# GAT and mixture-of-experts kernel, edge loop: order of weighing, adding, softmax and rescaling

## What is computed

```python
h   = einsum('nf,hfo->nho', layernorm(x), W)
e_s, e_d = einsum('nho,ho->nh', h, a_src), einsum('nho,ho->nh', h, a_dst)
scores = leaky_relu(e_s[src] + e_d[dst], 0.2)
m   = segment_max(scores, dst)                      # per node and head
ex  = exp(scores - m[dst])
agg = segment_sum(ex / segment_sum(ex)[dst] * h[src], dst)
x1  = x + relu(agg)
out = x1 + experts(layernorm(x1))                   # top 2 of 8, gelu between two layers
```

## Time and profile before

| | |
|---|---|
| median of 3 runs | 1369.36 us (1367.18 to 1370.95) |
| the profiled execution, own time | 1363.46 us |
| its span, first to last instruction | 1361.6 us |
| mean granted clock of TensorE | 0.745 |
| busy over the span: PE, DVE, POOL, ACT | 54%, 55%, 55%, 32% |
| instructions | 11490 |

### The profile page before, as it was taken

The page is one execution under the profiler, slowest core; times in us unless marked ns, Lnnn a source line. Parts: engine busy times, 40 slices in busy tenths (PEclk is TensorE's granted clock), DMA queues, the critical chain, the costliest instruction groups (busy, mean ns, idle before and its releaser), DMA issues.

```text
span 1361.6 us, 11490 instructions
## 1 busy us (share of the span) xinstructions
PE 730.0 (54%) x2620; PEld 543.7 (40%) x2620; DVE 744.5 (55%) x1862; ACT 429.8 (32%) x1157; POOL 751.7 (55%) x801
## 2 busy tenths in 40 slices
PE   7800324434445445443454455444446658999990
PEld 5600213323333333333343343333334555767770
DVE  7502334566556645666566456646667785444445
ACT  5331021432243314332432243224333263222220
POOL 2577746666666666666666666667650003444430
PEclk9855657777776776667766766777778758999995
DMA  6343423333333333333333333333328221111217
GB/s 195 84 115 105 109 66 97 97 99 97 98 99 93 92 97 95 95 97 101 98 90 97 95 94 96 96 97 101 94 79 288 68 78 51 67 63 66 64 46 238
DMA packets 77549, 136.04 MB, mean 100 GB/s; under 512 B 21953, under 2 KB 50081, under 8 KB 77355
## 3 DMA queue, kind: packets, MB, share of 16 engines
q0 software_dynamic: 37344, 101.67, 27.4%
q1 hardware_dynamic: 37401, 30.76, 7.4%
q10 hardware_dynamic: 2738, 2.88, 0.7%
HBM read 119.41 MB, written 16.48 MB: 100 GB/s over the span
## 4 chain that ended last, share of the span: by engine, by line
issue 35%; PE 18%; PEld 15%; DVE 15%; PEldq 11%; another core or an unknown queue 2%; DMA 1%; SPq 1%; DVEq 0%; ACT 0%; POOL 0%; POOLq 0%; ACTq 0%
PEld psum L673 15%; PEldq L675 11%; PE psum L763 6%; PE psum L785 6%; DVE acc L1183 2%; PE psum L622 2%; PE psum L775 2%; PE psum L715 1%; PE psum L752 1%; DVE links L1213 1%; DVE C L1223 1%; PE psum L706 1%; DVE acc L1530 1%; DVE acc L1531 1%
## 5 line engine op out<-in xcount | busy, mean ns | idle before, releaser
L546 POOL DMA_INDIRECT ring<-h_tab,srcP x664 | 631.3, 951 | 312.1 <-issue 191.4
L673 PE MATMUL psum<-ring,shared 128*128 128x260 f32 x1328 | 437.5, 497 | 492.9 <-issue 444.1
L673 PEld LDWEIGHTS psum<-ring,shared 128*128 128x128 f32 x1328 | 327.2, 254 | 593.2 <-issue 470.4
L1183 DVE TENSOR_TENSOR acc<-acc,psum 128x260 f32 x332 | 140.4, 423 | 297.8 <-PEq L675 238.3
L881 ACT ACTIVATE shared<-iota_f,Dcol 128x128 f32<-128x128 f32 x664 | 202.2, 386 | 159.8 <-PEq L675 143.6
L1270 DVE TENSOR_TENSOR ring<-ring,psum 128x2048 f32<-128x2048 f32 x83 | 189.8, 2287 | 34.1 <-remote 21.6
L899 ACT ACTIVATE Ex<-Z 128x128 f32<-128x128 f32 x21 | 6.5, 309 | 459.6 <-DVE Z L1237 251.7
L556 POOL DMA_INDIRECT ring<-z_tab,ring x47 | 45.1, 959 | 132.6 <-DVE ring L1473 118.6
L886 ACT ACTIVATE shared<-shared,ones 128x1024 f32<-128x1024 f32 x83 | 95.3, 1148 | 42.5 <-remote 32.1
L983 ACT ACTIVATE RS_all<-psum,tail_consts 128x128 f32<-128x128 f32 x188 | 53.7, 368 | 144.8 <-PE psum L775 144.8
L562 POOL DMA_INDIRECT ys_tab<-shared,ring x47 | 46.1, 980 | 94.7 <-DVE shared L1501 94.7
(11 more groups left out here) (296 smaller groups left out, 701.6 us busy)
## 6 DMA issues: line engine op xcount, KB each, us to landing
ring<-h_tab,srcP POOLq DMA_INDIRECT x664
ring<-in_L_ffn_W SPq DMA_DIRECT2D x16, 512.0 KB, 9.9
h_tab<-ring SPq DMA_DIRECT2D x10, 260.0 KB
ring<-in_x SPq DMA_DIRECT2D x1, 2432.0 KB
z_tab<-ring SPq DMA_DIRECT2D x2, 1024.0 KB, 4.4
ring<-ys_tab SPq DMA_DIRECT2D x4, 512.0 KB, 9.2
ring<-ys_tab ACTq DMA_DIRECT2D x4, 512.0 KB, 9.8
out<-acc SPq DMA_DIRECT2D x4, 512.0 KB
```

The source lines that it names most:

```text
L546: pool.indirect_dma_start(out=ring[:, t % RING, :], out_offset=None, in_=h_tab, in_offset=bass.IndirectOffsetOnAxis(ap=srcP[:, t:t + 1], a ...
L673: pe.matmul(sums[G_at % NSUM][:, 0:MW], dst_oh[:, n % OHB, 2 * g + r, :], ring[:, t % RING, :], start=(r == 0), stop=(r == 1))
L1183: v.tensor_tensor(a, a, sums[(n * GB + g) % NSUM][:, 0:MW], ALU.add).then_inc(flushed, 1)
```

## The change

In DVE's program all four batches of a phase are weighed, and three of them added, before the softmax product of the next phase begins. The flush of the last batch goes behind the first weigh of the next phase. `rescale` goes behind the third weigh, with a wait of its own for the phase's first batch. `gates` has one flush and the rescaling less ahead of it. PE's factor product goes behind the fourth batch, and ACT makes one more batch of one-hots ahead of the exponents. No instruction of arithmetic is added or removed.

```diff
 (PE)
                 batch(n + 2)
+                batch(n + 3)
                 if f < NPH - 2:
                     factor(f + 1)
-                batch(n + 3)
 (ACT)
                 lay_seeds(f + 2)
+                one_hots(n + 4)
                 exponents(f + 1)
-                one_hots(n + 4)
                 one_hots(n + 5)
 (DVE)
                 weigh(n)
                 if f:
-                    flush(n - 2)
+                    flush(n - 1)
                 weigh(n + 1)
-                if f:
-                    flush(n - 1)
-                    rescale(f)
                 gates(f + 1)
                 weigh(n + 2)
+                if f:
+                    v.wait_ge(batch_done, n + 1)
+                    rescale(f)
                 flush(n)
+                weigh(n + 3)
+                flush(n + 1)
+                flush(n + 2)
                 if f < NPH - 2:
                     weights(f + 1)
-                weigh(n + 3)
-                if f < NPH - 2:
                     factor(f + 1)
-                flush(n + 1)
-                if f < NPH - 2:
                     turn(f + 1)
             last = (NPH - 1) * PB
-            flush(last - 2)
-            flush(last - 1)
             weights(NPH - 1)
             factor(NPH - 1)
             turn(NPH - 1)
             weigh(last)
+            flush(last - 1)
             v.wait_ge(fac_in, 1)
             rescale(NPH - 1)
```

## The result

The changed kernel takes **1373.04 us** (median of 14 runs, 1367.97 to 1376.78), the kernel before on the same chip **1369.45 us** (14 runs): ratio **1.002, 95% interval 1.0011 to 1.003**. A second comparison, at a later time, gave 1367.49 against 1362.73 us, 1.0024 (1.0006 to 1.0041). The change costs about 0.2%; the forecast was 0.3% the other way. It lies in the forecast's range, within what I called no change, but the term that made the forecast a gain (the start, -10) came to nothing, and the other two came out otherwise too.

A forecast was written before the change was run, and what follows sets the result against it. The edge loop was taken as paced by waits: PE's marks held while POOL's gathers run. +4 - 10 + 1.5 = -4.5 us gave 1359.0, plus 5.9 to the median, 1364.9 us; range 1332 to 1400.

The forecast's parts named there:

- the start, -10: Start of the edge loop: second batch's mark comes at 186.3 instead of 196.3, 3 us after POOL's last gather; -10 us.
- the hold: Edge loop: while gathers run, a second PE batch's mark is not released until POOL stands still; mechanism unknown.
- Rival (c): Start of the loop: its loss only moves with phase 1's softmax to the new place; 1374.9 or 1370.9 us, chance 0.11.
- Loop, +4 us: Softmax moved behind the third batch's flush: mean cost 0.2 us in 20 phases, +4 us, ends 0 and +44.
- T + 20.3 to 25.0: Next phase's first batch done 20.3 to 25.0 us after T, when a phase's third batch is done; cover until 22.8.
- rival (a): Edge loop: the serial softmax chain becomes the bound, +22 to +44 us, giving 1383 to 1405 us; chance 0.34.
- the pairs of 22.8 us: Edge loop's usual cycle: two batches in 20 us of gathers plus about 2.8 us of POOL standstill.
- Rival (b): Edge loop: late first batch isn't held, POOL stands 1 us instead of 3; -40 us, about 1325; chance 0.19.
- Removed stall: PE's mid-batch stop for sum banks, flush behind softmax, eight times (34.5 us): removal worth 0 inside the loop.
- Tail, +1.5 us: After the last gathers: third batch ends earlier, but the last softmax starts at 1050.4 instead of 1048.86; +1.5 us.
- Gates, rescale's new wait, factor, SP: 0: Edge loop: earlier gates, rescale's added wait, PE's later factor product and SP's earlier-released loads each cost 0.
- the 60 us of the Trainium skill's rule: PE idle gaps halve the clock: by the rule alone 3 us a phase, 60 us more; left out of the sum.

The follow-up runs named there:

- experiment 7: The changed kernel once more, unaltered, measured beside the kernel before at a later time: 1367.49 against 1362.73 us, ratio 1.0024.

## Why the prediction was wrong

**Start, -10 us: the step that failed.** I wrote that the hold would end "3 us after POOL's last gather (183.3)". The cover that I named, DVE's crawl, was taken away as predicted: DVE had nothing beside the second batch from 165.6 us on and the softmax of phase 1 took 8.8 us. The mark came at 195.9 all the same, and POOL's wait is 12.33 instead of 13.12. The 3 us were no constant but the backlog of 16 gathers; 88 gathers make 12 to 13 us. Both numbers were in front of me: 2.8 / 16 = 0.18 and 12.8 / 88 = 0.15 us a gather, once the usual 0.3 us between gathers is taken off. I took the crawl beside the long standstill for its cause; with the crawl gone the standstill stayed, so it is not. Rival (c) had its result right (no gain at the start) and its reason wrong: the loss did not move with the softmax, it stayed where it was. That its 1374.9 us is so near to 1373.04 is luck, since its +4 and +1.5 came out as 0 to 3.4 and some +5.

**Loop, +4 us; measured 0 to 3.4.** The size is near, and the reasoning behind it was not. In the prediction the softmax would take 8.5 to 11 us and be hidden by 22.8 us of gathers. It took 13 to 18.5 in 11 of 17 phases, so the first batch, which I had done at T + 20.3 to 25.0, was done later than that in those (for T = 381.3: weighed at 406.6 and marked at 412.9, T + 31.6). By the sum of rival (a) that would be over +22 us. It isn't, for POOL's pace stays (559, 555, 559 and 555 gathers in 794 us in four traces), and batches that come late are caught up in threes. I took the pairs of 22.8 us for the law; they were the old order's habit, and what stayed is 1.42 us a gather. Rival (b) is excluded too: POOL's waits are 103 us, not under 80. By the marks the loop costs 3.4 us in one execution and nothing in the other.

**Removed stall: 0 in the loop** held. PE's waits for banks fell from 34.5 to 8.6 us, in 7 instead of 8 waits, and POOL's pace did not move. At the end the third batch is whole, as I expected (1019.94), while the second is split, with 1.41 us of waiting for DVE's adds instead of the 4.43 of before.

**Tail, +1.5 us; measured +4.7 and +5.7 from b75 to b82: the term that holds the loss.** PE of the changed kernel, 1011 to 1044 us:

```profile
1011.69 3.03 PE L673 MATMUL psum<-ring,shared 128*128 128x260 f32 x8 [2.00 <-DVE ring L1271]
1016.13 3.58 PE L673 MATMUL psum<-ring,shared 128*128 128x260 f32 x8 [1.41 <-DVE acc L1183]
1019.94 3.75 PE L673 MATMUL psum<-ring,shared 128*128 128x260 f32 x16 [0.23 <-issue]
1023.92 3.75 PE L673 MATMUL psum<-ring,shared 128*128 128x260 f32 x16 [0.23 <-issue]
1034.81 0.58 PE L662 MATMUL psum<-fm,oh_row 1*128 1x4 f32 x2 [7.15 <-DVE fm L1247]
1037.46 6.60 PE L673 MATMUL psum<-ring,shared 128*128 128x260 f32 x16 [2.07 <-DVE ring L1271]
```

and its DVE, the softmax of phase 19 and the weigh behind it:

```profile
1026.01 0.41 DVE L1205 STREAM_TRANSPOSE TB<-ring 128x128 f32<-128x128 f32 x1
...
1034.38 0.13 DVE L1242 COPY links<-links 12x1 f32<-12x1 f32 x1
...
1035.02 2.29 DVE L1270 TENSOR_TENSOR ring<-ring,psum 128x2048 f32<-128x2048 f32 x1
```

In the kernel before, the same softmax had run from 1002.85 to 1013.64, while gathers were still being issued, and PE went from b75 to b76 without a pause:

```profile
1022.85 3.77 PE L673 MATMUL psum<-ring,shared 128*128 128x260 f32 x16
1026.85 3.75 PE L673 MATMUL psum<-ring,shared 128*128 128x260 f32 x16 [0.23 <-issue]
```

In the changed kernel it waits for the flush of b74 and starts at 1026.01, 5.4 us after the last gather was issued (11.2 us in the second execution), with nothing left to cover it: PE stands from 1027.7 to 1037.46, and b76 then takes 6.60 us instead of 3.75 (granted clock 0.56 from 1037.5 to 1044; in the kernel before 1.00 from 1027 to 1030.6). The same 9.8 us are in the second execution (experiment 7) and in the kernel with half the gathers. Part comes back behind it: the last softmax has one flush less ahead of it, so that from b79 to b80 it is 15.1 us (16.1 in the second execution) instead of 20.4. The prediction had this softmax in its sum, but took b74 to end at 1017.6; it ended at 1023.7 and, in the second execution, at 1022.5, since the batches ahead of it stood later than before. So the last softmax started at 1055.93 and 1054.74 instead of 1050.4. The test that I had named for this term, the last softmax relative to the last gather, scatters too much to show it: 35.4 and 41.2 us, before 36.4.

**Gates, rescale's new wait, factor, SP: 0.** Nothing speaks against it: SP's loads are no releaser in any of the waits shown. It is not shown term by term, and the run made for ACT met the device without the hold.

**The sum.** -10 became 0, +4 became 0 to 3.4, +1.5 became some +5: 5.8 and 5.5 us in the marks of b82, +3.6 and +4.8 in the medians, against -4.5. The clock hardly entered: 0.73 against 0.72 over 216 to 1010 us, and the 60 us of the Trainium skill's rule did not appear. Nor does the Trainium skill's reading of a repeated gap in "Perfetto Trace Analysis", "Optimization Strategy" (that it can mean too few buffers) fit: POOL's standstills repeat 31 times from 216 to 1010 us, and giving it more lead (112) made the changed kernel 2% slower, less (56) 1.8% faster.

## What to carry to other kernels

When a producer's standstill is to be shortened, set its length against the work issued ahead of it at several places of the trace; if both grow together, it is more likely a backlog, and taking work from beside it need not help. A wait that disappears from one engine's list while the producer's count per stretch stays the same is no gain, so compare that count first. Compare two orders by several marks, and at the same place in the pattern: one batch can stand 9 us behind and the next but one 1. A chain that is covered in the loop has no cover behind the producer's last item, so work out the last round by itself. Under a fixed pace, the gain lies in what is still outstanding when the producer ends: try a shorter lead, and order the consumers so that they can live with it.

## What the hardware showed that I had not expected

- The device is in one of two conditions: 1227.46 us against 1369.99 us for the same program, at different times on one chip. In the faster one no mark is held and no DVE step crawls.
- With the hold, gathers are paced at 1.42 to 1.43 us over the loop, though POOL issues one in 1.25, and the number stays within 1.42 to 1.44 whether the lead of the changed kernel is 48, 56, 64 or 80, or PE has 100 us less to do.
- What is in arrears is not the gathers' data. While the kernel before waits for b1's mark at 196.1, POOL stands and the DMA engines move nothing (the last two numbers are their busy share and GB/s):

```profile
186.00:196.00 10.00, 0.00 (x0) 0.00 (x0) 2.10 (x9) 0.94 (x4) 0.00 (x0) 0.50 0.00 0
```

- The traces differ in what they hold of the gathers. In the kernel before the landings of all 664 are missing, as in every trace with the hold; in the four without it 320 to 504 of them are there, with a median of 2.8 us from issue to landing. The first line is of the kernel before, the second of the one with ACT's order undone:

```profile
ring<-h_tab,srcP POOLq DMA_INDIRECT x664
ring<-h_tab,srcP POOLq DMA_INDIRECT x664, 2.8
```

  So the hold comes together with lost records of semaphores. Whether one causes the other, or the recording itself has a part in the hold, no run here tells.
- The crawl keeps the same beat. At the start of the kernel before, three small additions of DVE and the transpose behind them begin 1.40 us apart, with 1.2 us of idling between:

```profile
176.45 0.20 DVE L1223 TENSOR_TENSOR C<-links 12x32 f32<-12x32 f32 x1 [2.56 <-issue]
177.85 0.21 DVE L1223 TENSOR_TENSOR C<-links 12x32 f32<-12x32 f32 x1 [1.20 <-issue]
179.26 0.21 DVE L1223 TENSOR_TENSOR C<-links 12x32 f32<-12x32 f32 x1 [1.20 <-issue]
180.65 0.21 DVE L1225 STREAM_TRANSPOSE carries<-C 128x32 f32<-128x32 f32 x1 [1.18 <-issue]
```

  That one gather and one DVE step take the same 1.4 us suggests that something handles the gathers' and the engines' signals one after another at 1.4 us a gather. This is argued from the equal beat and was not tested, and strict order alone doesn't give the marks: with a lead of 112, b1 was through at 165.3, when 74 gathers were issued, so its mark would be due at 72.8 + 74 x 1.4 = 176, and it came at 202.7. What the hold is, and why it was absent at one time, stays open.
